# Half of the second attention's key projections computed inside the first attention, with its transposed x kept as a ring of six tiles

## What is computed

```
# 1. first attention ("channel attention"): q, k from the context alone; it mixes the 512 channels
q = ctx @ Wq.T + bq;  k = ctx @ Wk.T + bk          # (4, 512, 128)
x = x + layernorm(x) @ softmax(q @ k.T).T
# 2. mixture of experts: 8 experts, top 2 per token, and a shared expert
x = x + moe(layernorm(x))
# 3. second attention: 16 heads of 128, 8 key/value heads (groups)
q2 = layernorm(x) @ Wq2                            # from x
k2 = ctx @ Wk2;  v2 = ctx @ Wv2                    # from the context alone, (4, 512, 8 * 128) each
x = x + softmax(q2 @ k2.T / sqrt(128)) @ v2 @ Wo
# 4. gated feed-forward with Hadamard transforms
x = x + ffn(layernorm(x))
```

## Time and profile before

| | |
|---|---|
| median of 3 runs | 2311.48 us (2311.15 to 2314.42) |
| profiled execution, its own time | 2312.58 us |
| its span (first to last instruction) | 2310.8 us |
| TensorE matmul busy | 2237.5 us, 97% of the span |
| VectorE / ScalarE / GpSimd busy | 62% / 46% / 20% |
| mean granted TensorE clock | 0.988 of full |

### The profile page before, as it was taken

The page is one execution under the profiler, slowest core; times in us unless marked ns, Lnnn a source line. Parts: engine busy times, 40 slices in busy tenths (PEclk is TensorE's granted clock), DMA queues, the critical chain, the costliest instruction groups (busy, mean ns, idle before and its releaser), DMA issues. The chain is left out here.

```text
span 2310.8 us, 32098 instructions
## 1 busy us (share of the span) xinstructions
PE 2237.5 (97%) x11073; PEld 1857.7 (80%) x11073; DVE 1436.8 (62%) x2985; ACT 1051.6 (46%) x1871; POOL 460.2 (20%) x441
## 2 busy tenths in 40 slices
PE   6989999998999999999999999999998999999999
PEld 4667788887999978788888888888877888888887
DVE  7864365535777763767767676767776555564544
ACT  4522120104566556666666666666664232322321
POOL 4503545401111172010001000010031302121000
PEclk8989999999999999999999999999999999999999
DMA  4331321115777785201011110001002232232331
GB/s 162 96 110 45 107 62 30 30 57 183 285 275 268 272 286 200 77 28 37 19 36 36 28 35 27 27 27 36 28 10 69 83 109 101 83 127 82 109 114 51
DMA packets 92507, 222.33 MB, mean 96 GB/s; under 512 B 9584, under 2 KB 30576, under 8 KB 89328
## 3 DMA queue, kind: packets, MB, share of 16 engines
q1 hardware_dynamic: 84080, 193.65, 24.4%
q0 software_dynamic: 8320, 27.27, 4.6%
HBM read 176.85 MB, written 44.04 MB: 96 GB/s over the span
## 5 line engine op out<-in xcount | busy, mean ns | idle before, releaser
L1899 ACT ACTIVATE route_weights<-route_weights,xa_minus_max 128x512 f32<-128x512 f32 x256 | 184.8, 722 | 193.0 <-DVE xa_minus_max L2047 192.9
L2063 DVE TENSOR_TENSOR xa_late_hi<-xa_ps_t,route_wv_hi 128x512 fp32r<-128x512 f32 x256 | 174.9, 683 | 128.8 <-ACT route_wv_hi L1908 128.6
L1834 POOL TENSOR_TENSOR route_kv_lo<-route_rows,route_kv_hi 128x1024 fp32r<-128x1024 f32 x32 | 76.9, 2403 | 729.3 <-ACT route_kv_hi L1873 729.3
L1908 ACT ACTIVATE route_wv_hi<-xa_ps_t 128x512 fp32r<-128x512 f32 x256 | 151.4, 592 | 106.9 <-PE xa_ps_t L2242 72.5
L2047 DVE CUSTOM_DVE_ANT_0 route_weights<-xa_ps_s,route_mask_bias 128x512 f32<-128x512 f32 x256 | 175.6, 686 | 1.1 <-issue 0.5
L2242 PEld LDWEIGHTS xa_ps_t<-ident,route_weights 128*128 128x128 f32 x1024 | 126.3, 140 | 44.0 <-issue 9.1
L2242 PE MATMUL xa_ps_t<-ident,route_weights 128*128 128x128 f32 x1024 | 153.8, 273 | 5.5 <-DVE xa_late_hi L2063 4.7
L2609 ACT ACTIVATE ffn_silu<-ffn_ps_gate,late_scales 128x512 f32<-128x512 f32 x64 | 44.2, 690 | 249.0 <-PE ffn_ps_gate L85 249.0
L83 PE MATMUL xa_ps_p<-route_wv_hi,route_kv_hi 128*128 128x512 f32 x284 | 118.2, 416 | 4.8 <-DVE xa_late_lo L2085 3.2
L881 ACT ACTIVATE moe_silu<-moe_ps_gate 128x512 f32<-128x512 f32 x44 | 26.2, 596 | 201.0 <-PE moe_ps_gate L85 201.0
L2425 DVE TENSOR_TENSOR route_kv_lo<-route_weights,route_kv_hi 128x1024 fp32r<-128x1024 f32 x42 | 53.7, 1279 | 101.8 <-ACT route_kv_hi L2420 101.7
(11 more groups left out here) (423 smaller groups left out, 6595.4 us busy)
## 6 DMA issues: line engine op xcount, KB each, us to landing
route_weights<-in_ffn_w SPq DMA_DIRECT2D x64, 512.0 KB, 3.7
route_weights<-in_expert_w SPq DMA_DIRECT2D x12, 1408.0 KB, 6.4
ex_w_raw<-in_expert_w SPq DMA_DIRECT2D x12, 1408.0 KB, 6.5
route_weights<-wd_folded SPq DMA_DIRECT2D x64, 256.0 KB, 2.6
moe_y<-ex_y SPq DMA_DIRECT2D x40, 256.0 KB, 3.5
route_weights<-in_xa_w SPq DMA_DIRECT2D x20, 512.0 KB, 3.7
route_weights<-in_expert_w SPq DMA_DIRECT2D x12, 768.0 KB, 9.0
ex_w_raw<-in_expert_w SPq DMA_DIRECT2D x12, 768.0 KB, 8.5
```

The source lines that it names most:

```text
L1834: pool.tensor_tensor(kvl[b % 2][:], rawkv[b % 2], f32(kvh[b % 2][:]), ALU.subtract).then_inc(M.kv_ready, 1)
L1899: act.activation(prob[slot][:], prob[slot][:], ACT.Exp, bias=nmx[:, slot:slot + 1], scale=-1.0, accum_out=tot[:, slot:slot + 1]).then_inc( ...
L1908: act.activation(PTh[:, :, tt * P:(tt + 1) * P], psT[tt % 2][:].rearrange("p (k n) -> p k n", k=TT), ACT.Copy).then_inc(M.pt_hi, 1)
L2063: dve.tensor_tensor(PTl[:, :, tt * P:(tt + 1) * P], psT[tt % 2][:].rearrange("p (k n) -> p k n", k=TT), f32(PTh[:, :, tt * P:(tt + 1) * P] ...
```

## The change

Four of the eight key groups (`EARLY_KEYS`) are now projected in the first attention: 16 units (4 batches x 4 groups), 6 matmuls each, at fixed places of its order. The context halves get four buffers there, for which the transposed x shrinks to a ring of six tiles. The stretch of units in the second attention falls from 64 to 48 and its tiles are turned after every second unit instead of every third.

```diff
+EARLY_KEYS = GROUPS // 2
...
+    RING = TT + 2
+    STAGES, PER = 4, EARLY_KEYS
+    KEYS_AFTER_SCORES = {-1: (0,), 0: (1,), 1: (2,), 2: (4,), 3: (7,), 4: (10,), 6: (11,), 7: (13,), 8: (15,)}
+    KEYS_AT_END = {1: (3,), 2: (5, 6), 3: (8, 9), 6: (12,), 7: (14,)}
+    KEYS = B * PER
+    CTX_STEPS = (1, 3)
+    KEYS_BEFORE_QK = {1: 1, 2: 11, 3: 16}
+    KEYS_IN_X = 8
...
-        ctxh, ctxl = ([sb(f"ctx_{n}{i}", [P, KV, S], F32R) for i in range(2)] for n in ("hi", "lo"))
+        ctxh, ctxl = ([sb(f"ctx_{n}{i}", [P, KV, S], F32R) for i in range(B)] for n in ("hi", "lo"))
+        stages = sb("key_stages", [P, STAGES, S], F32)
+        wkr = stages[:, 0:KV, :]
...
+        def key_bank(u):
+
+            return {1: psX, 2: psX, 4: psX, 7: psX, 6: psQ[1], 9: psQ[1], 12: psQ[1], 14: psQ[1]}.get(u, psQ[0])
...
+                        for k in range(KV):
+                            sp.dma_start(wkr[:, k, :].rearrange("p (g d) -> p g d", g=PER),
...
+                def store_key(u):
+                    b, g = divmod(u, PER)
+                    sp.wait_ge(M.key_out, u + 1)
+                    sp.dma_start(G.k_dram[g * B + b], stages[:, u % STAGES, :]).then_inc(key_stored[u % STAGES], 16)
...
+                pool.wait_ge(M.wk_hi, 1)
+                pool.tensor_tensor(wkl[:], wkr, f32(wkh[:]), ALU.subtract).then_inc(M.wk_ready, 1)
                 rstd(0)
...
-                    if tt == 2 and b + 2 < B:
-                        ctx_low(b + 2)
+                    if i in CTX_STEPS:
+                        ctx_low(CTX_STEPS.index(i) + 2)
...
+                def key_copy(u):
+                    act.wait_ge(M.key_done, u + 1)
...
+                    act.activation(stages[:, u % STAGES, :], key_bank(u)[:], ACT.Copy).then_inc(M.key_out, 1)
...
                 qk_high(0)
+                act.wait_ge(M.wk_loaded, 16 * KV)
+                act.activation(wkh[:], wkr, ACT.Copy).then_inc(M.wk_hi, 1)
...
+                    for u in KEYS_AT_END.get(i - 1, ()):
+                        key_copy(u)
                     if 0 <= n < NF:
                         wd_high(n)
...
+                        if i >= RING:
+                            act.wait_ge(M.x_done, i - RING + 1)
                         high(i)
+                        if i == 0:
+                            for u in KEYS_AFTER_SCORES[-1]:
+                                key_copy(u)
+                        for u in KEYS_AFTER_SCORES.get(i, ()):
+                            key_copy(u)
                         if i + 2 < NT:
                             exp(i + 2)
...
+                def key(u, i):
+
+                    b, g = divmod(u, PER)
+                    pe.wait_ge(M.ctx_ready, b + 1)
+                    pe.wait_ge(M.wk_ready, 1)
+                    if key_bank(u) is not psX:
+                        pe.wait_ge(M.qk_ready, 2 * (max(i - 1, 0) // TT) + (2 if i < 1 else 4))
+                    if key_before(u) is not None:
+                        pe.wait_ge(M.key_out, key_before(u) + 1)
...
+                for u in KEYS_AFTER_SCORES[-1]:
+                    key(u, -1)
...
+                    for u in KEYS_AFTER_SCORES.get(i, ()):
+                        key(u, i)
                     if 0 <= i - WD_LAG < NF:
                         wd(i - WD_LAG)
                     if i >= TT:
                         weighted(i - TT)
+                    for u in KEYS_AT_END.get(i, ()):
+                        key(u, i)
...
-        PER = 2 * TT + GROUPS
+        PER = 2 * TT + LATE_KEYS
         KVS = B * PER
         BEFORE_Q = KVS - 4
+        FIRST_TURN = KVS - 2 * NT - 1
...
-            return (n - PER) // 3 if n >= PER and n % 3 == (PER + 2) % 3 else None
+            return (n - FIRST_TURN) // 2 if n >= FIRST_TURN and (n - FIRST_TURN) % 2 == 0 and n < KVS - 1 else None
...
-                    if n == PER - 2:
+                    if n == FIRST_TURN - 1:
                         norm(0)
                         norm(1)
```

More of the change, by code:

```diff
@@ L301, in channel_attention @@
         wd_stored = [sem(f"wd_stored{i}") for i in range(2)]
+        key_stored = [sem(f"key_stored{i}") for i in range(STAGES)]
         M = Bag()
+        M.wk_loaded = sem("wk_loaded")
+        M.wk_hi = sem("wk_hi")
+        M.wk_ready = sem("wk_ready")
+        M.key_done = sem("key_done")
+        M.key_out = sem("key_out")
         M.ident_loaded = sem("ident_loaded")
@@ L332, in columns, with ring, xT_slot, key_before @@
             return ap.rearrange("p (k n) -> p k n", k=TT)
+        def ring(t):
+            return slice(t % RING * P, t % RING * P + P)
+        def xT_slot(t):
+            return R.xTh[:, :, ring(t)], R.xTl[:, :, ring(t)]
+        def key_bank(u):
+            return {1: psX, 2: psX, 4: psX, 7: psX, 6: psQ[1], 9: psQ[1], 12: psQ[1], 14: psQ[1]}.get(u, psQ[0])
+        def key_before(u):
+            return max([v for v in range(u) if key_bank(v) is key_bank(u)], default=None)
         with nc.Block() as block:
@@ L361, in _ @@
                         sp.dma_start(wds[n % 2][:], io["wdT"][n + 2]).then_inc(wd_loaded[n % 2], 16)
+                    for u in KEYS_AFTER_SCORES.get(n + 1, ()) + KEYS_AT_END.get(n + 1, ()):
+                        store_key(u)
                     sp.wait_ge(M.wd_out, n + 1)
@@ L365, in _ @@
                     sp.wait_ge(wd_stored[i], 16 * (NF // 2))
+                for i in range(STAGES):
+                    sp.wait_ge(key_stored[i], 16 * (KEYS // STAGES))
             @block.gpsimd
@@ L473, in _ @@
                         wd_out(n - 1)
-                    if tt == 2 and b + 2 < B:
-                        ctx_high(b + 2)
+                    if i in CTX_STEPS:
+                        ctx_high(CTX_STEPS.index(i) + 2)
             @block.vector
@@ L479, in _ @@
                 ch = Chain(dve, M.chain)
-                stats, norm, low = ln_vector(dve, R, x, xT_tile(R), lambda t: psT)
+                stats, norm, low = ln_vector(dve, R, x, xT_slot, lambda t: psT)
                 def qk_low(b):
@@ L602, in weighted @@
                         pe.wait_ge(M.x_added, t)
-                    tok = slice(t * P, (t + 1) * P)
+                    if t == 0:
+                        pe.wait_ge(M.key_out, KEYS_IN_X)
+                    tok = ring(t)
                     for k in range(KC):
@@ L1640, in cross_attention @@
         NW = KV * GROUPS * D
+        LATE_KEYS = GROUPS - EARLY_KEYS
+        NK = KV * LATE_KEYS * D
         HEAD = 2 * NW
@@ L1652, in cross_attention @@
         late_lo = sb("late_lo", [P, HEAD + 2 * S], F32R)
-        wkh, wvh = late_hi[:], G.wvh[:]
-        wkl, wvl = late_lo[:, 0:NW], late_lo[:, NW:HEAD]
-        PTh, PTl = (half.rearrange("p (k n) -> p k n", k=TT) for half in (wvh, wkh))
+        wkh, wvh = late_hi[:, 0:NK], G.wvh[:]
+        wkl, wvl = late_lo[:, 0:NK], late_lo[:, NW:HEAD]
+        PTh, PTl = (half.rearrange("p (k n) -> p k n", k=TT) for half in (wvh, late_hi[:]))
         o_hi, o_lo = ([late_lo[:, (i + n) * S:(i + n + 1) * S] for i in range(3)] for n in (0, 3))
@@ L1802, in _ @@
                     if n == BEFORE_Q - 8:
-                        for first in range(TT + 1):
+                        for first in range(TT):
                             stored(sp, first)
```

51 lines of the change are left out of this document (33 added, 18 removed).

## The result

Median of 13 runs each: 2305.03 us after (2301.42 to 2308.93), 2311.28 us before (2306.85 to 2314.42). That is 6.2 us faster in the medians. The ratio is 0.9976, or 0.24% faster, with a 95% interval of 0.9967 to 0.9985. The forecast was 2305.

A forecast was written before the change was run, and what follows sets the result against it. TensorE was taken to bound the unit stretch but to idle in the first attention. First attention +6.1, second attention -12.7: -6.6 us, 2306.0 from the profiled 2312.58, set to 2305 for the median; range 2297 to 2313, forecast's own 2301 to 2308.

The forecast's parts named there:

- level: Rival, chance 0.24: ScalarE's longer order or a longer third wait eats the gain; 2 to 3 us faster, 2309.
- The rival of the low clock: First attention, i = 0 to 4: small waits keep TensorE at 1.2 GHz; 5.4 us slower, 2317; chance 0.13.
- The TensorE-bound stretch: Rival, second attention: TensorE stays the bound, all 22.4 us come back; 16.3 us faster, 2295; chance 0.13.
- 12.7 back: Second attention: 22.4 us of units leave; after new waits for norm 13.7 come back, less 1.0 for low clock.
- The wait before turn 0: Unit stretch: turn 0 follows unit 15 at 843.1 and waits for `norm(0)` until 845.3, 2.1 us.
- the DMA share of 0.72: Second attention: this share was said to have slack after the last gather that covers the stores; no cost.
- The low clock behind the last wait: Unit stretch: half clock after the third new wait, ahead of turn 8; bounds 0 and 1.6 us, taken as 1.0.
- 12.1 us back: Second attention by the Trainium skill's rule: 1.6 us instead of 1.0 lost to the half clock after waits.
- 6.1 later: First attention: its end moves by this many us from the 16 added key units; bounds 3.6 and 18.
- `turn(1)` stays at 27.4: First attention's start: key units 0 and 1 fit into waits and time won from the clock, leaving this start unchanged.
- 0.5 earlier: First attention's start: the favorable bound in us for `turn(1)`; the other was 3 us later if the clock stays low.
- i = 6 to 8: First attention iterations with five keys: 23.9 us of TensorE work against 20.3 before; 3.7 paid, 3.1 go into waits.

The follow-up runs named there:

- one_gather: Changed kernel with one gather per token tile instead of two, its rows used twice (wrong result): unit stretch 82.1 us, profiled span 2296.9 us.
- after_again: The changed kernel unedited, run again: 2307.72 us (6 runs), 0.9964 of the kernel before; unit stretch 94.8 us.
- rstd_first_again: Second run of the changed kernel with GpSimd's rstd(b) ahead of the context low part of batch b + 1: 2301.29 us beside 2303.73 unedited.
- before_rstd_first: Kernel before the change with GpSimd's rstd(b) ahead of the context low part of batch b + 1: 2315.66 us against 2316.34, ratio 1.0002.

## Why the prediction was right

**Against the rivals.** Faster by 6.2 us: neither level, nor slower by the low clock, nor 2295. The rival of the low clock fails in the stretch it named, 1.00 where it wanted 0.50. The TensorE-bound stretch is what one_gather shows, and only it.

**The unit stretch.** Forecast 12.7 back, measured 13.6 in this profile; 104.0 less the mean of the three profiles of the changed kernel (91.7) is 12.3. Two of the three waits stood where GpSimd's clock had put them. `norm(4)` and `norm(8)` waited 6.8 and 5.1 us (forecast 8 and 5), TensorE 2.4 and 2.3 (3.3 and 2.8). The wait before turn 0 (forecast 2.1) was some 0.25. There I had kept the old 23.8 us from first unit to unit 16, and it took 25.2, since the low clock behind the stretch's first wait lasted longer than in the earlier trace rows: from 832 to 836 it was still 0.69. And `norm(0)` ended 0.7 us sooner after the first unit. Together 1.4 and 0.25 against 2.1: a term of the sum was wrong in name and nearly right in what it cost, and that was luck. The agreement to 0.9 us holds for this execution; in the other two the waits fell elsewhere (above), and the 94.8 of after_again comes from late copies, which the forecast had at nothing. It took the DMA share of 0.72 over the whole stretch as room for the stores, while in the stretch's first 22 us the share was 0.97 to 1.00 in all three.

**The low clock behind the last wait** I took at 1.0, with 1.6 as the upper bound. From turn 8 to turn 9 it took 889.73 - 884.88 = 4.85 us, against 3.23 where nothing disturbed (turns 5 to 6): 1.6, the bound. After turn 4 only 0.2 was lost. The rule of the Trainium skill (TensorE: Matmul & The Clock Gate, section "HAM oscillation — how this bites in real kernels"), that work between waits starts at the half clock each time, held for one of the two waits and for the one that counted. The case which that section describes has longer waits between its bursts than these. Its 12.1 us back would have been a little closer to the mean of 12.3 than my 12.7, too little to tell them apart. In rstd_first_again, whose longest such wait is 1.8 us, the clock over the stretch is 0.98 instead of 0.95.

**The first attention.** Forecast 6.1 later, measured 4.7 (5.9 and 5.4 in the other two profiles). By steps:

- "`turn(1)` stays at 27.4": it came at 24.7, the end of "0.5 earlier" and 2.2 beyond it. 0.7 of the 2.7 is the first context, which came sooner in this execution; the rest is mostly the clock, at 1.00 already from 17 us and not only behind 22. The 27.4 itself was one execution's value: before_rstd_first, with the same first attention, had `turn(1)` at 25.7 with no key in it.
- i = 1 then gave back 1.6 of that: 7.2 us instead of 5.6, since key 3 waited 1.8 us for VectorE's `qk_low(1)`, which came only 0.8 us sooner (28.09 instead of 28.89).
- i = 2 and 3: 6.5 and 6.2 (6.2 each). i = 4: 9.7 (10.3), as key 10 waited 0.5 for ScalarE and not 1.4: ScalarE, too, was ahead of where I had put it.
- i = 6 to 8: 83.19 - 59.05 = 24.1 us against 20.3, so 3.9 paid, 3.7 forecast. From there to the stage's end 49.0 us against 49.3, as good as nothing, as said.

The term that was off is the start, sized with rows taken at the low clock. Counted from TensorE's first matmul the first attention is 5.4 us longer in this execution (124.26 instead of 118.86) and 6.0 in the other two, so the 6.1 was better than the 4.7 makes it look.

**What I left out.** I forecast from two stages and took the rest as still. It isn't: the experts' 691 to 695 us in four profiles without the change and 690 to 696 in eight with it have means of 692.2 and 693.2. In the execution after it came to 696.2, of which 1.8 us lie ahead of the first expert matmul, which waited 8.4 us instead of 6.2 while the shared expert's weights took a median 7.8 us to land instead of 6.2. With the change this piece was 13.3 to 15.1 us, without 13.3 to 13.9. Whether the change causes about 1 us there is not settled. By the means of the profiles (three of the changed kernel, two of the one before) the first attention is 5.5 longer and the stretch 12.3 shorter: 6.8 faster, where the medians gave 6.2, 8.6 and 7.5.

## What to carry to other kernels

Moving work from a stage whose engine is full to one where it idles gives back its length less what the next in line takes: here 22 us of units became 12 to 14, as GpSimd's order, free until then, came to hold TensorE in two of three profiles. Walk the other engines' clock times past the shortened work before counting on the ceiling, and look for what stands needlessly ahead of the result that is now waited for: swapping two calls on GpSimd was worth nothing before the change and probably 2.4 to 3.2 us after it. And where TensorE idles before another engine's results and has come to the half clock, work put into those gaps costs less than its length, or nothing: here a quarter of it and nothing.

## What the hardware showed unexpectedly

- 6.8 us of added matmuls left the first attention as long as it was, and 18.2 us taken out shortened it by 4 to 5: the clock was 1.00 from 34.0 to 38.4 us with the added work in both kernels, and 0.50 to 0.75 without it.
- One kernel's copies waited for outside events between 0.7 and 11.6 us in all over the same stretch, in different executions, at a DMA share of about 1 in its first third. A single profile can't size a stretch of this kind to better than 5 us; the medians of 6 to 13 runs could.
- The half clock at the start of the unit stretch was gone at once in two of twelve executions and lasted over both of the first two units in four, in kernels of both kinds: 2.9 to 5.3 us for the same twelve matmuls.
